# First feed-forward block without GpSimd: down product in plain fp32, splits on ScalarE and VectorE

## The reference

```python
h = silu(x @ w_gate) * (x @ w_up)          # 1024 hidden units
g = h.reshape(B, S, I // 4, 4)
_, idx = top_k(abs(g), 2)                  # keep the 2 largest of every 4
h_sparse = (g * mask(idx)).reshape(B, S, I)
x = x + h_sparse @ w_down
```

## Time and profile before

| | us |
|---|---|
| median of 3 runs | 760.65 |
| lowest | 760.13 |
| profiled execution | 759.08 |
| its span, first to last instruction | 757.1 |

### The profile page before, as it was taken

How to read it: one execution, slowest core, us unless ns; L and a number is a source line. 1 busy time by engine, 2 the same in 40 slices (tenths; PEclk the granted TensorE clock), 3 DMA queues, 4 the chain that set the end, 5 groups by cost and what they waited for, 6 DMA issues and landing times.

```text
span 757.1 us, 15084 instructions
## 1 busy us (share of the span) xinstructions
PE 713.8 (94%) x4360; PEld 637.9 (84%) x4360; DVE 519.8 (69%) x1733; ACT 409.6 (54%) x1213; POOL 404.5 (53%) x545
## 2 busy tenths in 40 slices
PE   4899999999999989976889999999999999889998
PEld 3689999999999978765778999999999999877887
DVE  7898888888888877979876644444444545566533
ACT  3576676676676744521336556555555555545221
POOL 4898887887887866516468532415141325316000
PEclk9999999999999989989899999999999999999999
DMA  6010010101110110300101010101010200000000
GB/s 222 2 43 19 25 44 1 42 0 42 72 53 0 56 57 1 111 1 1 42 1 54 3 57 1 57 1 55 0 55 0 97 0 14 2 14 1 1 29 29
DMA packets 9004, 24.66 MB, mean 33 GB/s; under 512 B 896, under 2 KB 3072, under 8 KB 8832
## 3 DMA queue, kind: packets, MB, share of 16 engines
q1 hardware_dynamic: 8240, 22.55, 8.7%
q10 hardware_dynamic: 720, 1.57, 0.6%
HBM read 23.07 MB, written 1.05 MB: 32 GB/s over the span
## 4 chain that ended last, share of the span: by engine, by line
PE 86%; DVE 8%; issue 3%; POOL 1%; DMA 1%; ACT 1%; SPq 0%; DVEq 0%; ACTq 0%; POOLq 0%
PE bank L295 12%; PE bank L278 11%; PE bank L272 10%; PE bank L587 10%; PE bank L327 7%; PE bank L250 7%; PE bank L307 6%; PE bank L316 5%; PE bank L620 5%; PE bank L329 4%; PE bank L249 4%; PE bank L338 3%; DVE work L804 2%; PE bank L645 1%; DMA x<-in_x 1%
## 5 line engine op out<-in xcount | busy, mean ns | idle before, releaser
L398 ACT ACTIVATE probs<-scores,negmax 128x128 f32<-128x128 f32 (+1 forms) x256 | 115.5, 452 | 42.5 <-DVE negmax L446 41.9
L427 DVE TENSOR_TENSOR enc_lo<-bank,enc_hi 128x256 fp32r<-128x256 f32 x128 | 54.2, 424 | 121.7 <-PE bank L250 111.0
L351 ACT COPY probs_t<-bank 128x384 f32<-128x384 f32 x128 | 61.3, 479 | 128.5 <-PE bank L316 128.5
L490 POOL TENSOR_TENSOR a_hi<-raw_a,zero 128x384 fp32r<-128x384 f32 (+2 forms) x75 | 60.2, 803 | 109.1 <-PE bank L307 107.3
L410 DVE TENSOR_SCALAR probs<-probs,rinv 128x128 f32<-128x128 f32 (+1 forms) x256 | 86.7, 380 | 4.5
L295 PE MATMUL bank<-b_hi,enc_hi 128*128 128x256 f32 x256 | 75.4, 294 | 5.9 <-DVE x L418 5.9
L327 PE MATMUL bank<-probs_t,v 128*128 128x256 f32 x256 | 77.9, 386 | 1.3 <-DVE enc_lo L427 1.2
L250 PE MATMUL bank<-qk 128*128 128x256 f32 x256 | 77.4, 384 | 0.0
L492 POOL TENSOR_TENSOR a_lo<-raw_a,a_hi 128x384 fp32r<-128x384 f32 (+2 forms) x75 | 74.2, 989 | 5.9
L503 POOL TENSOR_TENSOR rms_r<-meansq,neg_half 128x3 f32<-128x3 f32 x64 | 58.1, 909 | 32.2 <-DVE meansq L480 32.0
L295 PE MATMUL bank<-b_hi,enc_lo 128*128 128x256 f32 x256 | 72.7, 284 | 0.0
(11 more groups left out here) (103 smaller groups left out, 2170.2 us busy)
## 6 DMA issues: line engine op xcount, KB each, us to landing
raw_a<-in_wa SPq DMA_DIRECT2D x10, 768.0 KB, 4.4
raw_a<-in_wa SPq DMA_DIRECT2D x9, 512.0 KB, 4.1
raw_b<-in_wb SPq DMA_DIRECT2D x16, 256.0 KB, 2.6
x<-in_x SPq DMA_DIRECT2D x4, 256.0 KB, 5.8
w_a<-in_w2t SPq DMA_DIRECT2D x1, 1024.0 KB, 4.8
raw_a<-in_wax SPq DMA_DIRECT2D x2, 512.0 KB, 3.3
raw_b<-in_wdown SPq DMA_DIRECT2D x2, 512.0 KB, 3.7
raw_a<-in_wa ACTq DMA_DIRECT2D x1, 512.0 KB, 4.7
```

The costliest lines, as they stand in the source:

```text
L398: nc.scalar.activation(probs[:, c % 4, c0:c1], scores[:, c % 2, c0:c1], ACT.Exp, bias=negmax[:, c % 2, r:r + 1], scale=-1.0, accum_out=row ...
L490: nc.gpsimd.tensor_tensor(hi, src, zero[:, 0:1].broadcast_to(list(src.shape)), ALU.add).then_inc(s_hi, 1)
```

## The change

The first feed-forward block uses GpSimd for the layer-norm `pow` alone.

- The down product takes the selected hidden tiles and the loaded `raw_b` as they are, in plain fp32: four matmul instructions for each token tile in place of twelve. `act_hi`, `pool_lo` and `dve_lo23` of this block are gone, and so are the four b pieces of the down weights.
- The hidden state gets its own tiles for k = 2 (a free part of v) and k = 3 (a new buffer of 8 KB for each partition); `squares` shares memory with `gate` to make room.
- Gate/up pieces 4 and 5 are split by ScalarE (hi) and VectorE (lo), behind the layer-norm steps of tile 6.
- The split of layer 1's first weights (four parts of 128x384) is on ScalarE (hi, ahead of silu 15) and VectorE (lo, behind hidden tile 15).
- SP loads the a weights of layer 1's pairs 0 and 1 earlier (a0 behind pieces 0 and 1, a1 behind pieces 4 and 5); the b weights of pairs 0 and 1 wait for the down product of k = 2 and of k = 3, since `raw_b` is now read by it.
- POOL, which had its part of the block ahead of its slots of layer 1, goes from four `pow` straight to slot -5.

```diff
@@ pe_down and pe_last_down
-                    pe.wait_ge(s["hi"], 4 * k + 4)
-                    if f == 0 and k >= 2:
-                        pe.wait_ge(s["lo"], 2 * k + 6)
-                        pe.wait_ge(s["lo23"], 2 * k - 2)
+                    if f == 0:
+                        pe.wait_ge(s["hs"], 4 * k + 4)
+                        if k < 2:
+                            pe.wait_ge(raw_bs[0][t], 16 * 5)
...
+                if f == 0:
+                    for j in range(4):
+                        mm = pe.matmul(bank[6 + d % 2][:, 0:D], hidden(0, k, j)[:, tt * P:(tt + 1) * P],
+                                       raw_b[:, t, j * D:(j + 1) * D], start=j == 0, stop=j == 3)
@@ act_ffn0
                 if k == 2:
-                    act_hi(act, 0, k)
+                    act_next_a(act)
                 act_silu(act, 0, i + 3)
                 act_abs(act, i + 2)
-                if k < 2:
-                    act_hi(act, 0, k)
@@ new on ScalarE and VectorE
+        def act_piece(act, n):
+            hi, _, source = piece_views(act, 0, n)
+            nc.scalar.copy(hi, source).then_inc(ff[0]["whi2"], 1)
+        def dve_piece(dve, n):
+            hi, lo, source = piece_views(dve, 0, n)
+            dve.wait_ge(ff[0]["whi2"], n - POOL_PIECES + 1)
+            nc.vector.tensor_tensor(lo, source, hi.bitcast(F32), ALU.subtract).then_inc(ff[0]["w2"], 1)
+        def act_next_a(act):
+            act.wait_ge(raw_as[1][0], 16)
+            act.wait_ge(ff[0]["up"], 12)
+            for part in range(4):
+                cs = slice(part * A0, (part + 1) * A0)
+                nc.scalar.copy(a_w[0][0][:, cs], raw_a[:, 0, cs]).then_inc(at[1]["a0hi"], 1)
+        def dve_next_a(dve):
+            for part in range(4):
+                cs = slice(part * A0, (part + 1) * A0)
+                dve.wait_ge(at[1]["a0hi"], part + 1)
+                nc.vector.tensor_tensor(a_w[0][1][:, cs], raw_a[:, 0, cs], a_w[0][0][:, cs].bitcast(F32),
+                                        ALU.subtract).then_inc(at[1]["a0"], 1)
@@ dve_ffn0
                     for t in range(4):
                         ln_dve_scale(dve, 2, t)
-                    dve_lo23(dve, 2)
                 dve_hidden(dve, 0, i + 3)
+            dve_next_a(dve)
             for t in range(4):
                 ln_dve_lo(dve, 2, t, LN2_BANK[t])
@@ SP
+                    if L == 1 and it is None and pair < 2:
+                        sp.wait_ge(ff[0]["down"], 12 + 4 * pair)
...
+                    load_a(None, 0)
+                    load_a(None, 1)
+                    load_b(None, 0)
+                    load_b(None, 1)
@@ GpSimd
-            for n in range(4, len(pieces[0])):
-                pool_piece(pool, 0, n)
-            pool_lo(pool, 0)
-            pool_lo(pool, 1)
-            pool.wait_ge(raw_as[1][0], 16)
-            pool.wait_ge(ff[0]["up"], 12)
-            w = WA[1] // 4
-            for part in range(4):
...
-                if part == 1:
-                    for t in range(4):
-                        ln_pool(pool, 2, t)
-                    pool_lo(pool, 2)
-            pool_lo(pool, 3)
+            for t in range(4):
+                ln_pool(pool, 2, t)
             slots(pool, 1, pool_slot, pool_head, pool_tail(pool, 1))
```

More of the change, by code:

```diff
@@ L156, in build @@
         raw_bs = [[sem(f"L{L}_raw_b{s}") for s in range(2)] for L in range(2)]
-        fnames = ("whi", "w", "gate", "up", "silu", "h", "abs", "cmp", "hs", "hi", "lo", "lo23", "down", "xadd")
+        fnames = ("whi", "w", "gate", "up", "silu", "h", "abs", "cmp", "hs", "hi", "lo", "whi2", "w2", "down", "xadd")
         ff = [{n: sem(f"F{f}_{n}") for n in fnames} for f in range(2)]
@@ L168, in ffn_pieces, with need_pieces @@
             ps += [("x1", "a", 1, main + c, c, 11) for c in range(0, rest, 512)]
-            ps += [(f"b{s}", "b", s, c, c, 8 + s) for s in range(2) for c in (0, 512)]
+            if f == 1:
+                ps += [(f"b{s}", "b", s, c, c, 8 + s) for s in range(2) for c in (0, 512)]
             return ps
         pieces = [ffn_pieces(f) for f in range(2)]
+        POOL_PIECES = 4
         def pieces_until(f, last):
             return max(i + 1 for i, p in enumerate(pieces[f]) if p[0] == last)
+        def need_pieces(eng, f, last):
+            n = pieces_until(f, last)
+            if f == 0 and n > POOL_PIECES:
+                eng.wait_ge(ff[0]["w2"], n - POOL_PIECES)
+            else:
+                eng.wait_ge(ff[f]["w"], n)
         def ln_dve_bn(dve, st, t):
@@ L366, in act_slot @@
                     need(act, s["ss"], it, m)
-                    nc.scalar.activation(squares[:, :], bank[PJ_BANK + m % 2][:, 0:384], ACT.Square).then_inc(s["sq"], 1)
+                    nc.scalar.activation(squares, bank[PJ_BANK + m % 2][:, 0:384], ACT.Square).then_inc(s["sq"], 1)
                     need(act, s["pv"], it, m - t % 2 - 14)
@@ L382, in act_slot @@
                         act.wait_ge(ff[0]["cmp"], 24)
+                    elif it is None and m == 8:
+                        act.wait_ge(ff[0]["down"], 12)
                     nc.scalar.copy(v[:, m // 8 % 2, t, :], bank[TQ_BANK][:, 0:D]).then_inc(s["vev"], 1)
@@ L599, in pe_gate_up, with hidden @@
                         ln_pe(pe, 2 * f + 1, tile, 6 + tile % 2)
+        def hidden(f, k, j):
+            return hid_late[k - 2][:, j, :] if f == 0 and k >= 2 else hid[:, k % 2, j, :]
         def pe_down(pe, f, k, tiles=range(4)):
@@ L725, in act_abs @@
                 act.wait_ge(ff[0]["cmp"], 6 * k)
-            nc.scalar.activation(mag[:, j, :], hid[:, k % 2, j, :], ACT.Abs).then_inc(ff[0]["abs"], 1)
+            nc.scalar.activation(mag[:, j, :], hidden(0, k, j), ACT.Abs).then_inc(ff[0]["abs"], 1)
         def act_ffn0(act):
@@ L770, in dve_hidden @@
                 dve.wait_ge(at[f]["scores"], UNITS)
-            if k >= 2:
+            if i == 8 and f == 0:
+                dve.wait_ge(at[0]["pv"], UNITS)
+            if k >= 2 and f == 1:
                 dve.wait_ge(s["hi"], 4 * k - 8 + j + 1)
                 dve.wait_ge(s["lo"], 4 * k - 8 + j + 1)
-            nc.vector.tensor_tensor(hid[:, k % 2, j, :], bank[2 * (i % 3) + 1][:, :], gate[:, i % 2, :],
+            nc.vector.tensor_tensor(hidden(f, k, j), bank[2 * (i % 3) + 1][:, :], gate[:, i % 2, :],
                                     ALU.mult).then_inc(s["h"], 1)
@@ L984, in load, with load_b @@
                         sp.dma_start(raw_a[:, slot, 0:WA[L]], wa[L][n]).then_inc(raw_as[L][slot], 16)
+                def load_b(it, pair):
+                    slot = pair % 2
+                    n = pair if it is None else it * 2 + pair
+                    if L == 1 and it is None and pair < 2:
+                        sp.wait_ge(ff[0]["down"], 12 + 4 * pair)
                     if it is not None or pair < PAIRS:
@@ L987, in load @@
                         sp.dma_start(raw_b[:, slot, 0:WB], wb[L][n]).then_inc(raw_bs[L][slot], 16)
-                for pair in range(4):
-                    load(None, pair)
+                def load(it, pair):
+                    load_a(it, pair)
+                    load_b(it, pair)
+                if L == 0:
+                    load(None, 0)
+                    load(None, 1)
+                else:
+                    load_a(None, 0)
+                    load_a(None, 1)
+                    load_b(None, 0)
+                    load_b(None, 1)
+                load(None, 2)
+                load(None, 3)
                 with sp.Fori(0, 2) as it:
```

131 lines of the change are left out of this document (60 added, 71 removed).

## The result

| | before | after |
|---|---|---|
| median us | 760.39 (4 runs) | 739.9 (4 runs, 737.93 to 740.67) |
| profiled execution us | 759.08 | 740.21 |
| its span us | 757.1 | 738.4 |
| mean granted clock | 0.982 | 0.993 |

The ratio is 0.9732 with a 95% interval of 0.9705 to 0.9759: faster. On the scale of the prediction's 760.65 us that is 740.3 us, at the lower edge of the forecast range (740 to 752, forecast 744.8); the median itself lies 0.1 us under that edge. One of the four runs of the kernel before took 2498 us; without it their median would be 760.13.

What follows compares the result with a forecast made beforehand. The prediction had TensorE and DVE sharing the bound in the first feed-forward block. 20.6 - 3.0 (pause) - 1.7 (clock) = 15.9 us off 759.08 gives 743.2, plus 1.57 to the median 744.8 us; range 740 to 752 us.

Steps and rivals of the forecast that it cites:

- The bound changes from DVE to TensorE: First feed-forward block: TensorE unbroken from 291 to about 354; last down product ends 20.6 us earlier before pauses.
- the walk: TensorE's and DVE's queues followed together: tile i = 15 finished at 349.7, only 0.2 us pause before it.
- The comparisons become fast: DVE's comparisons in the block, no longer beside POOL's splits: 1.2 to 1.3 us a pair throughout.
- The new collision: DVE's four subtractions behind hidden tile 15 meet POOL's splits: 4.7 us; TensorE pauses 3.0 us before d = 10.
- The clock: Behind the 3.0 us pause in the down product of k = 2, TensorE may run at half speed: 1.7 us taken.
- the likeliest case: Rival 2, the forecast with the pause and a clock price of 0 to 3.4 us: 743.1 to 746.5 us, chance 0.62.
- Outside the block: After the last down product the sequence to 396.33 is unchanged, and the second layer keeps its length.
- The sum: Whole kernel: 20.6 - 3.0 - 1.7 = 15.9 us gained, 744.8 us on the median's scale.
- No collision: Rival 1: POOL's splits slip past DVE's subtractions, so 20.6 - 0.2 us gained: 740.2 us, chance 0.12.
- the slow comparisons were not POOL's: Rival 4: DVE's comparisons are slow for another reason and DVE stays the bound: about 760 us, chance 0.05.
- the half clock in plain fp32: Rival 5: long plain fp32 runs don't get 2.4 GHz, 0.85 us a product: 771.7 us, chance 0.05.

Runs made afterwards that it cites:

- twice: The changed kernel with 48 of its 64 plain products issued a second time: 758.76 us, ratio 1.0032.
- poolwork: The changed kernel with three groups of four POOL subtractions added that nothing in the block waits for: 751.52 us, ratio 0.9944.
- late: The changed kernel with POOL's first split of slot -5 waiting for the six comparisons of k = 3: 738.05 us, ratio 0.9741.
- again2: The changed kernel unaltered, run once more on one chip beside order2b: 740.74 us, ratio 0.978.
- again: The changed kernel unaltered, run once more as base for edits around its pause: 740.06 us, ratio 0.9768.
- poolnext: The changed kernel with the split of layer 1's first weights returned to POOL: 741.63 us, ratio 0.9803.
- order2b: Second run of order2, on one chip beside the changed kernel (again2): 737.86 us, ratio 0.9747.
- order2: The changed kernel with DVE's four subtractions in pairs behind the residual additions of d = 8 and 9, ahead of the comparisons: 737.47 us, ratio 0.975.
- half: The changed kernel without hidden tiles 2 and 3 in the down products of k = 0 to 2, for timing only: 735.82 us, ratio 0.9736.

## Why the prediction was right, and where its terms were off

**The bound changes from DVE to TensorE.** Right. The pieces lie where the walk put them, shifted by the 1.1 us by which this execution entered the block later: tile 4 to 10 without a pause, three down products at 6.91, 7.15 and (without its pause) 7.2 us against 6.9, 7.1 and 6.9 foreseen. 64 products at 0.43 us was read off one row of attention and held over 14 us of such products in `twice`. 6.91 against 5.75 us is a ratio of 1.20, as the rows had it. The four passes that the Trainium skill gives ("FP8 and Floating Point Precision", section "TensorE Precision Notes"), set against three, would make 4/3; the trace doesn't agree with that as a price.

**The comparisons become fast.** Right: the 24 of the block now take 0.68 us each (684 ns at the median, 0.60 from the start of one to the next), the longest 687 ns, where before a group of four ran at 1.6 us each. `poolwork` shows the cause, which before had only been argued from times that coincide.

**The new collision.** Right in place and mechanism, and near in size. The timeline of DVE, then of POOL, after:

```profile
351.80 4.31 DVE L890 TENSOR_TENSOR a_lo<-raw_a,a_hi 128x384 fp32r<-128x384 f32 x4
356.04 1.41 DVE L239 TENSOR_TENSOR xT_lo<-bank,xT_hi 128x256 fp32r<-128x256 f32 x4
```

```profile
351.23 0.83 POOL L506 TENSOR_TENSOR a_hi<-raw_a,zero 128x384 fp32r<-128x384 f32 x1 [2.20 <-PE bank L601]
352.14 1.20 POOL L508 TENSOR_TENSOR a_lo<-raw_a,a_hi 128x384 fp32r<-128x384 f32 x1
353.30 1.14 POOL L506 TENSOR_TENSOR a_hi<-raw_a,zero 128x384 fp32r<-128x384 f32 x1
354.51 1.19 POOL L508 TENSOR_TENSOR a_lo<-raw_a,a_hi 128x384 fp32r<-128x384 f32 x1
```

4.2 us for the four against 4.7 foreseen and 1.87 without POOL (`late`); the pause 2.4 us against 3.0.

**The clock.** This is the term that was mis-sized. I took 1.7 us for a fall of the clock behind the pause. In the profiled execution it didn't fall. Busy time by window around the pause, after and then in `again2`, columns as in the earlier trace rows:

```profile
355.40:357.80 2.40, 0.02 (x1) 0.00 (x0) 2.40 (x7) 0.00 (x0) 0.30 (x1) 1.00 0.00 0
357.80:361.50 3.70, 3.67 (x17) 3.26 (x18) 3.70 (x8) 0.00 (x0) 0.00 (x0) 1.00 0.00 0
```

```profile
355.70:358.10 2.40, 0.01 (x1) 0.00 (x0) 2.40 (x7) 0.00 (x0) 0.29 (x1) 1.00 0.00 0
358.10:363.50 5.40, 5.38 (x17) 4.46 (x18) 4.24 (x8) 0.00 (x0) 0.00 (x0) 0.68 0.00 0
```

The same program with the same pause of 2.4 us went on at 1.00 here and in `again`, and at 1.2 GHz for part of the next 5.4 us in another execution; there the eight products behind the pause take 5.41 us in place of 3.72 and the stretch is 74.43 us, 1.7 longer. So the fall is real, costs what I gave it, and comes in some executions only: of three profiled ones, in one. As a term of the likeliest case it should have been nearly nothing. (`poolwork` has the same pause of 2.4 us ahead of 369.1 us, and `poolnext` one of 2.3: the clock stayed at 1.00 behind both.)

**Outside the block.** I held the second layer to its old length. From the end of the last down product to the end of the span it took 757.1 - 391.27 = 365.8 us before and 738.4 - 374.34 = 364.1 after, and the block was entered 1.1 us later. Neither need belong to the change. The block's first gate/up tile starts at 292.15 us in the profile after, at 289.90 in `again` and at 292.46 in `again2`, which are the same kernel. And a fall of the clock of 3.4 us near 662 us in the profile before is missing in the two profiles of the changed kernel that show 364.1, and is there (near 645 us) in those of `order2b` and `again2`, which show 365.7 and 365.8. That both move by execution is shown; what decides it isn't.

**The sum.** Forecast 15.9 us: 20.6 less 3.0 for the pause and 1.7 for the clock. Measured in the stretch 90.80 - 72.76 = 18.0: 20.7, as `order2`'s stretch of 70.08 gives it, less 2.7 for the pause. Outside of it 1.8 won and 1.1 lost: 18.7 us of span. Between the medians of the first measurement lie 760.39 - 739.9 = 20.5 us, 4.6 more than forecast: 1.7 is the clock, 0.3 the pause, 0.1 TensorE's work, 0.7 the parts outside, 0.2 the time outside the span, and 1.6 is that I added the distance between profiled execution and median of the kernel before (1.57 us) to the changed one, whose median lies 0.3 us below its profiled execution (and the one before now 1.3 above). So the result stands at the edge of the range, a good quarter more gain than forecast, and only the clock's term and the pause's are mechanisms of the change; the rest is, as far as these runs show, scatter between executions. Beside the kernel before in the later runs the gain was 15 to 18 us at the median, since that kernel itself came out at 756 to 758 us: that the forecast of 15.9 lies among these says little, since they hold the same scatter.

**The rivals.** No collision (740.2 us) is what the median looks like, but for another reason: the collision is there. That the slow comparisons were not POOL's is refuted by `poolwork`, the half clock in plain fp32 by `twice`.

## What to carry to other kernels

Before pricing a removed instruction, look at what it slowed on the other engine: here the splits cost TensorE nothing and ACT little, and yet removing them made the stretch 18 us shorter, 12.5 of them (by `poolwork`) because DVE's two-input instructions on SBUF stood beside them at two to three times their price and TensorE waited for DVE, in part with a clock that fell behind the wait. A product that is 20% dearer on TensorE is a good trade while another engine bounds the block, up to the point where the other engine is just hidden; `half` shows that this point is near here: of 10.3 us of TensorE's work left out, 3.8 come back. And work that moves to a freed engine, or that a freed engine starts earlier, has to be laid beside what the others do at that time: order DVE's queue so that residual additions which free PSUM banks come first, and place the two-input work where the other engine is idle.

## What I had not expected of the hardware

- **DVE and POOL don't always alternate.** In `poolwork`'s second group DVE's four comparisons ran at full speed (2.49 us), and POOL's first instruction, begun beside them at 319.02, took 3.48 us, the longest of the twelve (median 1.72). In the first and third group the slow alternation set in with the second comparison. The order of arrival doesn't tell them apart: in all three groups POOL's first instruction begins 0.16 to 0.23 us after DVE's first comparison (304.07 after 303.84, 319.02 after 318.85, 340.01 after 339.85). What decides is open. The page "SBUF — State Buffer" of the Trainium skill, section "SBUF: two separate sides", has the loser blocked for the whole instruction; that a queue of instructions back to back can hold POOL off for several is what this trace adds.
- **Counts suffer more than selections.** Beside POOL, counts of two bf16 tiles took 1.05 us in place of 0.335 (`late`), a factor of three, while selections, which also read two tiles of SBUF, kept to 673 to 690 ns in all thirteen profiles; in the kernel before, POOL's first lo tile at 317.56 us fell beside the selections of 316.09 to 318.5 and took 2.18 us itself, the longest of its kind. One more selection stands beside such a tile, at 382.70 in the same profile, and took 0.68 us too. Whether they are free of the conflict or were always first isn't settled by these runs.
- **Behind one and the same pause the clock may fall or not.** The granted clock stayed at 1.00 behind the pause of 2.4 us in two profiled executions of the changed kernel and fell in one, with nothing changed in the program.
